# Sequence 0 of a transformer kernel in two halves, its first half ahead with PSUM banks of its own, weights split in gaps, and the first feed-forward tile begun with half a sequence

## The chip, the core and the metric

One NeuronCore of one Trainium2 chip runs the whole program. It has five engines that run side by side and meet at semaphores: TensorE (PE), VectorE (DVE), ScalarE (ACT), GpSimd (POOL) and SyncE (SP, which only issues DMAs here). Each takes its instructions in the order of the program. The metric is the device time of one execution in microseconds, the median of several runs.

## What is computed

There are four sequences of 1024 tokens with 128 features each. The first layer is a block of its own; then come a feed-forward layer, an attention layer, and the same feed-forward layer again. Cut to what matters here (the attention layer is left out, since the change doesn't touch it):

```python
def conv_pool_block(x):                      # layer 1, on layernorm(x)
    h = ln(x, ln_conv_g, ln_conv_b)
    x = x + causal_conv(h, conv_w, 4 taps, 4 groups) + conv_b
    h = ln(x, ln_attn_g, ln_attn_b)
    q, k, v = h @ Wq.T + bq, h @ Wk.T + bk, h @ Wv.T + bv
    pooled_q = cumsum(q, axis=1) / scale     # scale = 1 .. 1024
    pooled_k = cumsum(pooled_q * k, axis=1) / scale
    x = x + pooled_k * v
    h = ln(x, ln_boom_g, ln_boom_b)
    h = gelu(h @ Wb.T + bb)                  # 512 wide
    return x + h @ Wu.T + bu

x = x + conv_pool_block(layernorm(x))
x = x + ffn(layernorm(x))                    # sum over 8 experts of (silu(x@wg) * (x@wu)) @ wd
x = x + attention(layernorm(x))
x = x + ffn(layernorm(x))
```

## The kernel before

Tokens are cut into 8 tiles of 512 (`NT`), two to a sequence, so a sequence is a pair of tiles; a tile is four blocks of 128 tokens. The kernel has three parts in time: a front that takes sequence 0 through layer 1 alone; the first feed-forward layer over four pairs of tiles, with layer 1 of sequence i+1 woven into pair i; and the rest (attention, then the second feed-forward layer beside it), which the change doesn't touch.

**Layer 1 of a sequence** is a chain of named stages, each done for half u = 0 and half u = 1 (512 tokens each). `sequence_step(b, p)` exists once for each engine, and does at position p what the table `AT` puts there. In order: `tok` (normalise tokens), `T1` (PE turns them so that features are the partitions), `copy`, `conv`, `a1`, `T5`, `stats5` (DVE statistics, then four small POOL instructions in `inner_norm`), `norm5`, `T7`, `h2`, then `q`, `cumq` (a running sum on DVE), `k`, `kq`, `cumk`, `v`, `vq`, with POOL's products by the reciprocal positions `rinv` between them, `T9`, `stats9`, `norm9`, `T10`, `h3`, `up` (four matmuls to 512 hidden features), `gelu`, `down` (four back), `y`, `T13`, `x1` (added to `x`). The running sums bind half 1 to the last column of half 0. The chain has PSUM banks 5 and 6 (half u uses bank 5 + u, and the other one in places), so one half's stage waits until the bank is read out.

**The front before** runs these positions for sequence 0 with nothing beside it on PE. Beside it the feed-forward weights are made ready: each of the three 128 x 4096 matrices is needed as a high part `w_hi` (an fp32r rounding, ACT) and a low part `w_lo` (the difference, POOL or DVE). They come in four quarters r = 0 to 3 of 1024 columns (three DMAs a quarter into `raw`), split at positions `SPLIT_AT`: ACT makes all high parts, POOL the low parts of quarters 0 to 2, DVE those of quarter 3. PE waits for all twelve low parts ahead of the first tile. DVE also takes the statistics of sequences 1 to 3 in the front, and POOL their roots (`norms_of_input`).

**The feed-forward layer** has 32 chunks of 128 hidden columns a tile. `pair(i, last)` runs 64 chunks: `gate_up` (three fp32r matmuls each for gate and up) two chunks ahead, `silu` on ACT, `product` on DVE, `h_hi` on ACT, `h_lo` on DVE, and `down` (three matmuls). `NORM_AT` says at which chunk the next tile is normalised. All engines ran pairs 0 to 2 in a hardware loop (`Fori`), and pair 3 written out. One pair takes chunks p = 0 to 63, and position p of sequence i+1 goes with chunk p.

## Time and profile before

| | |
|---|---|
| median of three runs (lowest to highest) | 1820.72 us (1818.81 to 1822.73) |
| the profiled execution, its own time | 1818.75 us |
| its span from first to last instruction | 1817.0 us |
| PE busy | 1704.4 us, 94% of the span |
| DVE, ACT, POOL busy | 69%, 57%, 26% |
| mean granted TensorE clock | 0.982 of full |
| first matmul of the first feed-forward tile | 104.75 us |

The span is cut into the front (0 to 104.75 us), four pairs of some 173 us, and the attention and second feed-forward part. A row of a timeline has the start, the length, the engine, the source line, the operation and its operands; what stands in brackets at its end is the idle time of the engine ahead of it and who ended it. The chain view follows the end of the program back through whatever released each step. A count such as x8 merges equal instructions; the length is then from the first start to the last end. An fp32 matmul of 512 columns shows as two records.

### The profile page before, as it was taken

To read this page: it belongs to the slowest core of one execution; us is meant where nothing else is said; L and a number is where in the kernel's file an instruction comes from. 1 tells how busy PE (TensorE), PEld (TensorE's weight loads), DVE (VectorE), ACT (ScalarE), POOL (GpSimd) and SP (SyncE) were. 2 spreads that over 40 slices of the span, in tenths; PEclk is the share of its full clock that TensorE was granted. 3 is DMA by queue.
4 is the path that set the end of the run, shared out by engine and by line. 5 is a ranking of instruction groups with operands and counts; after the bars stand their busy time and mean duration, and the time that the engine had idled before them with its cause. 6 is when DMAs were issued, how large, how long until landed. Compare 5 with 4: busy or idle time off the path is not lost.

```text
span 1817.0 us, 28722 instructions
## 1 busy us (share of the span) xinstructions
PE 1704.4 (94%) x10264; PEld 1106.2 (61%) x10264; DVE 1250.0 (69%) x2118; ACT 1040.8 (57%) x1694; POOL 477.6 (26%) x651
## 2 busy tenths in 40 slices
PE   4489999999999999988889999999999999999998
PEld 2257777767776877653334555555555555557877
DVE  3558566856675777777777777777777777746665
ACT  3435655574556555456666666556666566665554
POOL 4712000200020012432113444344444344440000
PEclk8699999999999999989999999999999999999999
DMA  5100000000000013232200010000000000010000
GB/s 173 39 1 1 1 1 1 0 0 0 1 0 0 1 61 106 82 100 82 59 25 25 24 36 2 24 24 13 25 23 25 2 24 2 3 30 1 6 7 6
DMA packets 60522, 47.01 MB, mean 26 GB/s; under 512 B 7647, under 2 KB 58222, under 8 KB 60398
## 3 DMA queue, kind: packets, MB, share of 16 engines
q1 hardware_dynamic: 60224, 45.33, 8.5%
q8 instruction: 73, 1.20, 0.3%
q14 instruction: 51, 0.42, 0.1%
q10 hardware_dynamic: 174, 0.07, 0.0%
HBM read 28.20 MB, written 17.17 MB: 25 GB/s over the span
## 4 chain that ended last, share of the span: by engine, by line
PE 83%; DVE 8%; ACT 4%; issue 3%; POOL 2%; DMA 0%; ACTq 0%; DVEq 0%; POOLq 0%
PE ps L1105 8%; PE ps L1068 7%; PE ps L1106 6%; PE ps L1107 6%; PE ps L969 6%; PE ps L971 6%; PE ps L970 6%; PE ps L942 4%; PE ps L1137 4%; PE ps L762 4%; PE ps L911 3%; PE ps L1139 3%; PE ps L1138 3%; PE ps L976 3%; PE ps L977 3%
## 5 line engine op out<-in xcount | busy, mean ns | idle before, releaser
L1434 ACT ACTIVATE pr<-ps 128x1024 f32<-128x1024 f32 (+2 forms) x285 | 267.8, 945 | 187.7 <-PE ps L899 115.7
L1841 DVE TENSOR_TENSOR hid<-sg,ps 128x512 f32<-128x512 f32 x256 | 174.8, 683 | 199.4 <-PE ps L971 155.4
L722 POOL TENSOR_TENSOR h_lo<-hid,h_hi 128x512 fp32r<-128x512 f32 x176 | 225.7, 1282 | 263.5 <-ACT h_hi L1530 259.0
L1440 ACT ACTIVATE sg<-ps 128x512 f32<-128x512 f32 x256 | 153.2, 599 | 244.7 <-PE ps L971 242.6
L1831 DVE TENSOR_REDUCE negp<-ps 128x2 f32<-128x1024 f32 (+2 forms) x224 | 254.6, 1145 | 49.9 <-PE ps L899 29.4
L969 PE MATMUL ps<-xn_hi,w_hi 128*128 128x512 f32 x512 | 226.5, 442 | 1.4 <-DVE xn_lo L1680 1.4
L1105 PE MATMUL ps<-xn_hi,w_hi 128*128 128x512 f32 x512 | 223.3, 436 | 0.7 <-DVE hid L1963 0.5
L1963 DVE SCALAR_TENSOR_TENSOR hid<-sg,ps 128x512 f32<-128x512 f32 x176 | 120.9, 687 | 126.2 <-ACT sg L1520 125.5
L971 PE MATMUL ps<-xn_hi,w_lo 128*128 128x512 f32 x512 | 202.0, 394 | 0.0
L1106 PE MATMUL ps<-xn_lo,w_hi 128*128 128x512 f32 x512 | 201.8, 394 | 0.0
L970 PE MATMUL ps<-xn_lo,w_hi 128*128 128x512 f32 x512 | 201.5, 393 | 0.0
L1107 PE MATMUL ps<-xn_hi,w_lo 128*128 128x512 f32 x512 | 201.3, 393 | 0.0
L1861 DVE TENSOR_TENSOR h_lo<-hid,h_hi 128x512 fp32r<-128x512 f32 x236 | 173.1, 733 | 0.0
L1530 ACT CAST h_hi<-hid 128x512 fp32r<-128x512 f32 x256 | 157.5, 615 | 14.7 <-PE ps L1139 10.2
L1457 ACT CAST h_hi<-hid 128x512 fp32r<-128x512 f32 x256 | 157.3, 614 | 0.6 <-DVE hid L1841 0.4
L1520 ACT ACTIVATE sg<-ps 128x512 f32<-128x512 f32 x176 | 105.4, 599 | 76.8 <-PE ps L1107 75.5
L1068 PE MATMUL ps<-pr,vp 128*9 128x512 f32 (+3 forms) x1376 | 145.3, 495 | 0.0
L942 PEld LDWEIGHTS ps<-qs,ks 63*128 63x128 bf16 x720 | 35.1, 94 | 166.8 <-issue 141.7
L942 PE MATMUL ps<-qs,ks 63*128 63x512 bf16 (+2 forms) x720 | 114.6, 336 | 13.5 <-DVE negp L1831 8.6
L1969 DVE TENSOR_TENSOR hid<-hid,ps 128x512 f32<-128x512 f32 x176 | 120.2, 683 | 6.7 <-PE ps L1107 3.1
L1105 PEld LDWEIGHTS ps<-xn_hi,w_hi 128*128 128x128 f32 x512 | 95.9, 187 | 40.3 <-issue 18.7
L911 PE MATMUL ps<-ks,qs 60*128 60x512 bf16 (+2 forms) x720 | 113.5, 331 | 6.1 <-DVE xn_lo L1953 2.6
(223 smaller groups left out, 3089.9 us busy)
## 6 DMA issues: line engine op xcount, KB each, us to landing
qs<-qd SPq DMA_DIRECT2D x60, 96.0 KB
ks<-kd SPq DMA_DIRECT2D x60, 96.0 KB
kd<-qkp SPq DMA_DIRECT2D x14, 256.0 KB, 2.9
qd<-qkp SPq DMA_DIRECT2D x7, 384.0 KB, 2.6
x<-in_hidden SPq DMA_DIRECT2D x4, 512.0 KB, 6.7
raw<-in_Wg SPq DMA_DIRECT2D x4, 512.0 KB, 4.4
raw<-in_Wu SPq DMA_DIRECT2D x4, 512.0 KB, 5.4
raw<-in_Wd SPq DMA_DIRECT2D x4, 512.0 KB, 6.7
```

Of the source, the lines that this page charges most:

```text
L722: g.tensor_tensor(h_lo[:, q % 2, :], hid[:, q % 4, :], h_hi[:, q % 2, :].bitcast(F32), ALU.subtract).then_inc(FS[1]["hlo_pool"], 1)
L942: mm = pe.matmul(dst[e], k_of(n)[r, hp, j * P:(j + 1) * P], q_of(n)[r, hp, from_q:from_q + w], start=True, stop=st not in MASKED)
L969: pe.matmul(dst, w_hi[m][:, w], xn_hi[:, h, :], start=True, stop=False)
L970: pe.matmul(dst, w_hi[m][:, w], xn_lo[:, h, :], start=False, stop=False)
L971: pe.matmul(dst, w_lo[m][:, w], xn_hi[:, h, :], start=False, stop=True).then_inc(f[sig], 1)
L1068: mm = pe.matmul(ps[32 * h:32 * h + HD + 1, O_BANK, from_q:NT], vp[:, n % 2, j, h, :], pr_of(n, st)[:, h, 0:NT - from_q], start=(j == 0), ...
L1105: pe.matmul(dst, w_hi[m][:, w], xn_hi[:, h, :], start=True, stop=False)
L1106: pe.matmul(dst, w_hi[m][:, w], xn_lo[:, h, :], start=False, stop=False)
L1107: pe.matmul(dst, w_lo[m][:, w], xn_hi[:, h, :], start=False, stop=True).then_inc(f[sig], 1)
L1434: a.activation(pr_of(n, st)[:].rearrange("p (e a) q -> p e a q", e=2)[:, :, hps[0]:hps[-1] + 1, 0:WIDTH[st]], heads(buf, hps, WIDTH[st]), ...
L1831: v.tensor_reduce(to[:, :, hps[0]:hps[-1] + 1, i % SUB], heads(buf, hps, JOB_WIDTH[k]), AX.X, ALU.max, negate=True).then_inc(T["reduced"], 1)
L1841: v.tensor_tensor(hid[:, c % 4, :], sg[:, c % 2, :], bank(2 + c % 2), ALU.mult).then_inc(f["prod"], 1)
```

## The change

**Order.** In the front each engine now has sequence 0's stages written out one by one (`first_step(name, u)`), half 0 ahead of half 1. Half 0 (called `ahead` in the code) has banks 0, 1 and 4 of its own, banks 0 to 3 for its four `up` matmuls, and a tile `gel_first` into which ACT puts the gelu with the bias in one instruction for each matmul. The feed-forward begins when half 0 is through: half 1's last stages (`up`, the gelu, `down`, `y`, `T13`, `x1`) stand around the first chunks. Pair 0 is written out as well (the loop has pairs 1 and 2), with sequence 1's positions six chunks later (`SHIFT_FIRST`) and tile 2's norm at chunk 20 of the second half.

**Loads and setup.** `x` of sequence 0 comes as two DMAs of 256 KB, and the other sequences' `x` after the small matrices and two quarters of the weights. There are two root chains of 4 blocks for sequence 0 where there was one of 8. ACT, not POOL, spreads the convolution weights. The reciprocal of the positions is taken in four quarters.

**Weights.** The low parts of quarter 0 are POOL's (two) and DVE's (one); those of quarter 1 are DVE's; those of quarters 2 and 3 are POOL's, quarter 3 inside pair 0. PE no longer waits for all twelve, but for quarter 0 ahead of the tile and for quarter r ahead of chunk 8r.

The constants, SP's queue, and POOL:

```diff
-NORM_AT = (10, 16)
...
-SPLIT_AT = (5, 10, 19, 27)
+SHIFT_FIRST = 6
+NORM_AT = {"first": (10, 20), "middle": (10, 16), "last": (13, None)}
+HIGH_LATE = 5
...
-                    sp.wait_ge(s["split_lo"], (r - 1) * 3)
+            def load_weights(r):
                 for m in range(3):
                     n = 2 if m < 2 else BLK
-                    sp.dma_start(raw[r % 2][m][:, :].rearrange("p (n f) -> p n f", n=n),
-                                 ffn_src[m][:, r * n:(r + 1) * n, :]).then_inc(s[f"raw_loaded{r % 2}"], 16)
+                    sp.dma_start(raw[r][m][:, :].rearrange("p (n f) -> p n f", n=n),
+                                 ffn_src[m][:, r * n:(r + 1) * n, :]).then_inc(s[f"raw_loaded{min(r, 1)}"], 16)
+
+            load_weights(0)
+            load_weights(1)
+            for b in range(1, B):
+                sp.dma_start(xs(b * BLK, BLK).rearrange("p (n d) -> p n d", d=D),
+                             x_blk[:, b * BLK:(b + 1) * BLK, :]).then_inc(s["x_rest_loaded"], 16)
+            for r in (2, 3):
+                sp.wait_ge(s[f"split_lo{r - 1}"], 3)
+                load_weights(r)
             attention_loads(sp)
...
+            def low_part(r, m):
+                pool.wait_ge(s[f"split_hi{r}"], m + 1)
+                g.tensor_tensor(w_lo[m][:, r * S:(r + 1) * S], raw[r][m][:],
+                                w_hi[m][:, r * S:(r + 1) * S].bitcast(F32), ALU.subtract).then_inc(s[f"split_lo{r}"], 1)
+
+            norms_of_input(0, SUB)
+            norms_of_input(SUB, BLK)
+            low_part(0, 0)
+            low_part(0, 1)
+            sequence_step(0, only("stats5", 0))
+            sequence_step(0, only("stats5", 1))
+            pool.wait_ge(s["rinv_ready"], 3)
+            sequence_step(0, only("cumq", 0))
+            sequence_step(0, only("cumk", 0))
+            sequence_step(0, only("vq", 0))
+            pool.wait_ge(s["rinv_ready"], 5)
+            sequence_step(0, only("cumq", 1))
+            sequence_step(0, only("stats9", 0))
+            sequence_step(0, only("cumk", 1))
+            sequence_step(0, only("vq", 1))
+            sequence_step(0, only("stats9", 1))

...
+                low_part(2, 0)
+                low_part(2, 1)
                 norm(0)
-                with pool.Fori(0, TILES // 2 - 1) as i:
-                    for p in range(2 * CH):
-                        sequence_step(i + 1, p)
-                        if p % CH == NORM_AT[p // CH]:
-                            norm(i * 2 + (p // CH + 1))
+                low_part(2, 2)
+                norms_of_input(BLK, B * BLK)
+                for m in range(3):
+                    low_part(3, m)
+                pair(0, "first")
```

PE, the front's order and the start of the tile:

```diff
+            for t in range(T_CONV, T_IN):
+                weight_T(t)
+            pe.wait_ge(s["small_loaded"], 16 * N_SMALL)
+            pe.transpose(bank(2)[:, 0:PAR_ROWS], prow[:, :],
+                         ident[0:PAR_ROWS, 0:PAR_ROWS]).then_inc(s["par_T"], 1)
+            for t in range(T_COUNT):
+                if not T_CONV <= t < T_IN:
+                    mm = weight_T(t)
             mm.then_inc(s["wraw_T"], 1)
-            pe.transpose(bank(7)[:, 0:PAR_ROWS], prow[:, :], ident[0:PAR_ROWS, 0:PAR_ROWS]).then_inc(s["par_T"], 1)
...
-            for p in range(AT["T1"][0] + 1, 2 * CH):
-                sequence_step(0, p, first=True)
+            first_step("T1", 0)
+            first_step("conv", 0)
+            first_step("T1", 1)
+            first_step("T5", 0)
+            first_step("conv", 1)
+            first_step("T7", 0)
+            first_step("T5", 1)
+            first_step("q", 0)
+            first_step("k", 0)
+            first_step("v", 0)
+            first_step("T7", 1)
+            first_step("q", 1)
+            first_step("k", 1)
+            first_step("T9", 0)
+            first_step("v", 1)
+            first_step("T10", 0)
+            for c in range(4):
+                first_step("up", 0, c)
+            first_step("T9", 1)
+            for c in range(4):
+                first_step("down", 0, c)
+            first_step("T13", 0)
+            first_step("T10", 1)
+            first_step("up", 1, 0)
+            first_step("up", 1, 1)

...
+                                if kind == "first" and p + 2 in (8, 16, 24):
+                                    pe.wait_ge(s[f"split_lo{(p + 2) // 8}"], 3)
                                 gate_up(h if c + 2 < CH else 1 - h, (c + 2) % CH)
...
                 transpose4(bank(7), ntok).then_inc(f["xT"], 1)
+                first_step("up", 1, 2)
+                first_step("up", 1, 3)
+                pe.wait_ge(s["split_lo0"], 3)
                 pe.wait_ge(f["xlo"], 1)
                 gate_up(0, 0)
                 gate_up(0, 1)
-                with pe.Fori(0, TILES // 2 - 1) as i:
-                    pair(i, False)
-                pair(TILES // 2 - 1, True)
+                for c in range(4):
+                    first_step("down", 1, c)
+                pair(0, "first")
+                with pe.Fori(1, TILES // 2 - 1) as i:
```

ACT and DVE, the front's order and what stands in the first pair:

```diff
+            act.wait_ge(s["par_ready"], 1)
+            first_step("copy", 0)
+            projections()
+            first_step("tok", 1)
+            for m in range(3):
+                high_part(0, m)
+            first_step("copy", 1)
+            first_step("h2", 0)
+            for m in range(3):
+                high_part(1, m)
+            first_step("norm5", 1)
+            first_step("h2", 1)
+            first_step("h3", 0)
+            for c in range(4):
+                first_step("up", 0, c)
+            for m in range(3):
+                high_part(2, m)
+            first_step("norm9", 1)
+            first_step("h3", 1)

...
                                 act.wait_ge(f["xT"], t + 2)
                                 split_input(1 - h)
+                            if kind == "first" and HIGH_LATE <= h * CH + c < HIGH_LATE + 3:
+                                high_part(3, c - HIGH_LATE)
...
                 split_input(0)
+                first_step("gelu", 1)
                 act.wait_ge(f["gate"], 1)
                 silu(0)
...
+            for u in range(2):
+                dve.wait_ge(s[f"x_loaded{u}"], 16)
+                stats_of_input(u * SUB, u * SUB + SUB)
+            positions()
+            quarter_of_positions(0)
...
+            first_step("tok", 1)
+            projections()
+            quarter_of_positions(3)
+            dve.wait_ge(s["par_ready"], 1)
+            first_step("a1", 0)
+            first_step("copy", 1)
+            first_step("stats5", 0)
+            low_part(0, 2)
+            first_step("norm5", 0)
+            first_step("a1", 1)
+            first_step("stats5", 1)
+            first_step("cumq", 0)
+            low_part(1, 0)
+            first_step("kq", 0)
+            first_step("cumk", 0)
+            low_part(1, 1)
+            first_step("vq", 0)
+            first_step("cumq", 1)
+            low_part(1, 2)
+            first_step("stats9", 0)
+            first_step("kq", 1)
+            first_step("norm9", 0)
+            first_step("cumk", 1)
+            first_step("vq", 1)
+            dve.wait_ge(s["x_rest_loaded"], 16 * (B - 1))
+            stats_of_input(BLK, 2 * BLK + SUB)
+            first_step("stats9", 1)
+            stats_of_input(2 * BLK + SUB, B * BLK)
+            first_step("y", 0)
+            first_step("x1", 0)
+            dve.wait_ge(s["a_x1"], 1)
+            first_norm(FS[0], 0)
+            first_norm(FS[0], 3)
+            first_step("hid1", 1, 0)
+            first_step("hid1", 1, 1)
...
+                                first_step(("y", "x1")[c], 1)
+                            if kind == "first" and h * CH + c == SHIFT_FIRST:
+                                dve.wait_ge(s["a_lnx"], 28)
                             if not last:
-                                sequence_step(i + 1, h * CH + c)
```

What this does to the engines' queues is seen at three places. On PE, the end of the front and the first chunks, before (ps is PSUM, work holds the hidden activations, a0T the transposed sequence):

```order
L831 MATMUL ps<-h2T,wt 128x512 x8
L838 MATMUL ps<-work,wt 128x512 x4
L762 MATMUL ps<-ident,a0T 128x128 x4
L838 MATMUL ps<-work,wt 128x512 x4
L762 MATMUL ps<-ident,a0T 128x128 x4
L762 MATMUL ps<-ident,ntok 128x128 x4
L969 MATMUL ps<-xn_hi,w_hi 128x512
```

and now:

```order
L872 MATMUL ps<-h2T,wt 128x512 x4
L793 MATMUL ps<-ident,a0T 128x128 x4
L881 MATMUL ps<-gel_first,wt 128x512 x4
L793 MATMUL ps<-ident,a0T 128x128 x4
L793 MATMUL ps<-ident,work 128x128 x4
L872 MATMUL ps<-h2T,wt 128x512 x2
L793 MATMUL ps<-ident,ntok 128x128 x4
L872 MATMUL ps<-h2T,wt 128x512 x2
L1041 MATMUL ps<-xn_hi,w_hi 128x512
```

The tile's transposes (ntok) stand before half 1's last two `up` matmuls, and half 1's four `down` matmuls and its T13 have moved behind the first chunks. On POOL, the pooling products of the front (L613, L616, L620) and the low parts of quarters 1 and 2, before:

```order
L633 TENSOR_TENSOR w_lo<-raw,w_hi 128x1024 x3
L613 TENSOR_TENSOR work<-work,rinv 128x512
L616 TENSOR_TENSOR work<-work,rinv 128x512
L613 TENSOR_TENSOR work<-work,rinv 128x512
L633 TENSOR_TENSOR w_lo<-raw,w_hi 128x1024 x3
L620 TENSOR_TENSOR a0T<-a0T,work 128x512
L616 TENSOR_TENSOR work<-work,rinv 128x512
```

and now:

```order
L628 TENSOR_TENSOR work<-work,rinv 128x512
L631 TENSOR_TENSOR work<-work,rinv 128x512
L635 TENSOR_TENSOR a0T<-a0T,work 128x512
L628 TENSOR_TENSOR work<-work,rinv 128x512
L613 TENSOR_TENSOR lna<-mva,eps 128x4
L614 TENSOR_TENSOR lna<-lna,half 128x4
L615 TENSOR_TENSOR lna<-mva,lna 128x4
L616 TENSOR_TENSOR lna<-zeros,lna 128x4
L631 TENSOR_TENSOR work<-work,rinv 128x512
L635 TENSOR_TENSOR a0T<-a0T,work 128x512
```

No low part stands between the pooling products any more, and half 0's second root (L613 to L616) stands ahead of half 1's products. On DVE, the last instructions ahead of the first product (`hid`), now:

```order
L1900 SCALAR_TENSOR_TENSOR a0T<-ps,par,a0T 128x512
L1904 TENSOR_TENSOR x<-x,ps 128x512
L1784 BN_STATS st<-x 128x6 x4
L1786 MEMSET fence 128x1
L1788 BN_AGGR mv<-st 128x2 x4
L1792 TENSOR_SCALAR ntok<-x,mv,lnw 128x128 x4
L1896 TENSOR_SCALAR work<-ps,par 128x512 x2
L2057 MEMSET x 128x512
L2058 MEMSET ps 128x512
L1807 TENSOR_TENSOR xn_lo<-ps,xn_hi 128x512
L1896 TENSOR_SCALAR work<-ps,par 128x512 x2
L2007 TENSOR_TENSOR hid<-sg,ps 128x512 x2
```

Half 1's hidden columns (L1896) stand around the first tile's xn_lo, where before they were done long ahead of it.

## Rows read from the trace of the kernel before

**Rows 1.** The page: busy time of the engines.

```profile
PE 1704.4 (94%) x10264; PEld 1106.2 (61%) x10264; DVE 1250.0 (69%) x2118; ACT 1040.8 (57%) x1694; POOL 477.6 (26%) x651
```

**Rows 2.** Windows: stretch, length, busy (count) by engine, PEclk, DMA share, GB/s.

```profile
0.00:104.75 104.75, 50.00 (x140) 25.62 (x140) 48.89 (x155) 38.25 (x60) 58.80 (x70) 0.80 0.31 92
104.75:281.84 177.09, 173.93 (x720) 129.26 (x721) 114.66 (x224) 99.17 (x176) 16.57 (x26) 0.99 0.00 1
26.00:33.00 7.00, 6.12 (x13) 3.17 (x12) 0.69 (x1) 5.57 (x7) 1.82 (x1) 0.50 0.00 0
62.00:84.00 22.00, 8.01 (x21) 4.79 (x22) 11.59 (x69) 5.61 (x12) 12.71 (x15) 0.50 0.01 1
105.50:108.40 2.90, 2.90 (x8) 2.30 (x7) 0.69 (x1) 0.60 (x1) 0.00 (x0) 0.50 0.00 0
```

**Rows 3.** The chain that ended last, 0 to 110 us: start, length, what.

```profile
0.81 4.97 DMA x<-in_hidden
...
28.27 9.70 PE ps L785 x16
...
54.17 1.24 DVE work L1741
...
58.05 7.82 POOL w_lo L633 x3
...
80.19 9.61 PE ps L831 x16
...
90.72 3.69 PE ps L838 x8
...
104.01 0.70 DVE xn_lo L1680
...
104.75 0.50 PE ps L969
```

**Rows 4.** Timeline of PE.

```profile
16.01 1.94 PE L762 MATMUL ps<-ident,work 128*128 128x128 f32 x8 [16.01 <-DVE work L1710]
...
123.87 3.60 PE L785 MATMUL ps<-hT,wt 128*128 128x512 f32 x8
```

**Rows 5.** Timeline of DVE.

```profile
68.29 0.89 DVE L1694 BATCH_NORM_STATS2 sta<-ps 128x6 f32<-128x128 f32 x4 [6.86 <-PE ps L762]
...
163.31 0.68 DVE L1861 TENSOR_TENSOR h_lo<-hid,h_hi 128x512 fp32r<-128x512 f32 x1
...
168.75 1.40 DVE L1861 TENSOR_TENSOR h_lo<-hid,h_hi 128x512 fp32r<-128x512 f32 x1
```

**Rows 6.** Timeline of POOL.

```profile
44.33 6.97 POOL L633 TENSOR_TENSOR w_lo<-raw,w_hi 128x1024 fp32r<-128x1024 f32 x3
51.59 1.26 POOL L613 TENSOR_TENSOR work<-work,rinv 128x512 f32<-128x512 f32 x1 [0.29 <-DVE work L1728]
...
69.68 0.20 POOL L598 TENSOR_TENSOR lna<-mva,eps 128x4 f32<-128x4 f32 x1 [1.37 <-DVE mva L1698]
69.96 1.02 POOL L599 TENSOR_TENSOR lna<-lna,half 128x4 f32<-128x4 f32 x1
...
83.17 5.04 POOL L576 TENSOR_TENSOR lnx<-tmpx,half 128x24 f32<-128x24 f32 x1
...
168.33 1.27 POOL L613 TENSOR_TENSOR work<-work,rinv 128x512 f32<-128x512 f32 x1 [1.82 <-DVE work L1728]
```

**Rows 7.** Timeline of ACT.

```profile
21.03 1.95 ACT L1345 COPY wt<-ps 128x512 f32<-128x512 f32 x4 [3.63 <-PE ps L857]
...
90.60 1.91 ACT L1390 ACTIVATE work<-work 128x2048 f32<-128x2048 f32 x1 [0.75 <-DVE work L1756]
...
103.99 1.28 ACT L1440 ACT_TABLE_LOAD   x1
106.13 0.60 ACT L1440 ACTIVATE sg<-ps 128x512 f32<-128x512 f32 x1 [0.85 <-PE ps L971]
```

**Rows 8.** DMA traffic between 2.5 and 10 us.

```profile
DMA packets 4355, 2.18 MB, mean 291 GB/s; under 512 B 100, under 2 KB 4355, under 8 KB 4355
```

More of the change, by code:

```diff
@@ L242, in build @@
         with ExitStack() as one:
+            sb("under_gelu", [P, 3 * S], F32, one)
+            gel_first = sb("gel_first", [P, 4, NT], F32, one)
+        with ExitStack() as one:
             v_first = sb("v_first", [P, BLK, D], F32, one)
@@ L1012, in pair @@
                                 maxima_T(0)
-                            if c == norm_at(h, last) + 4 and not end:
+                            if not end and c == NORM_AT[kind][h] + 4:
                                 pe.wait_ge(f["xadd"], t + 1)
@@ L1330, in attention @@
                 rest_of_ffn()
-            pe.wait_ge(s["split_lo"], 12)
             ffn(FS[0])
@@ L1891, in ffn @@
                 product(0)
-                with dve.Fori(0, TILES // 2 - 1) as i:
-                    pair(i, False)
-                pair(TILES // 2 - 1, True)
+                pair(0, "first")
+                with dve.Fori(1, TILES // 2 - 1) as i:
+                    pair(i, "middle")
+                pair(TILES // 2 - 1, "last")
                 dve.wait_ge(G["rest"], LAST * 2)
```

407 lines of the change are left out of this document (219 added, 188 removed).

## The prediction

> **What bounds the kernel now.** I read the page first: PE is busy for 94% of the span [rows 1], so outside the front only less PE work or less waiting could help. The windows then show where PE does wait. In the front, 0 to 104.75 us, it is busy for 50.0 of 104.75 us, and in the first pair for 173.9 of 177.1 [rows 2]. So there is a pool of some 55 us that lies almost whole in the front, and the change works on the front. The chain shows what the front consists of [rows 3]: eight convolution matmuls together (9.70 us), the pooling chain that goes from engine to engine, 7.82 us of POOL's low parts of the weights in the midst of it, then eight `up` matmuls (9.61), two times four `down` (3.69 for the first), and the feed-forward's first matmul at 104.75. All of that is done for both halves of the sequence before a tile begins, though the tile needs one half. The windows also give the clock: the granted clock stands at 0.50, that is 1.2 GHz, in 26 to 33, in 62 to 84 and again in 105.5 to 108.4 us [rows 2], after stretches in which PE was idle or sparse. At 1.2 GHz an fp32 matmul of 512 columns takes some 1.7 us; at 2.4 GHz four of them take 3.60 or less, 0.86 each [rows 4].
>
> **The walk through the new front.** The price of the new front is an order, so I walk through it, each instruction with its row's duration, 0.05 to 0.1 us for a hand-over, and each engine in its program order. The times are of half 0's chain.
> - Loads. In 2.5 to 10 us the queues move 291 GB/s [rows 8], and 512 KB of x land at 5.78 [rows 3]. The small matrices (0.98 MB) have 0.52 MB of x ahead of them, not 2.1 MB: with 1.5 us from last byte to signal they land at 9.2. x's first 256 KB land at about 4.9, and its root chain on POOL is through at 10.6.
> - Weights. PE has 16 transposes behind the load, then 8 for T1, 1.94 for eight [rows 4]: 13.0 and 14. ACT's four copies (1.95 [rows 7]) end at 15.1, `hT` at 15.9.
> - `conv` of half 0: four matmuls, 3.4 us at 2.4 GHz, to 19.4; `a1` to 20.3; T5 behind half 1's T1 to 20.9; statistics (1.4 us from the first statistics at 68.29 to POOL's start at 69.68 [rows 5, 6]) behind a copy, to 22.5. POOL is then in quarter 0's two low parts (6.97 us for three [rows 6]) until 23.9, and its root (0.2 + 1.02 [rows 6]) is there at 25.3. `norm5` on DVE to 26.4, T7, `h2`, and `q` starts at 27.9.
> - Pooling. The running sum waits for half 1's statistics on DVE, to 30.3; POOL's product (1.26 [rows 6]) waits for half 1's root and ends at 32.7; `kq`, `cumk` (1.24 [rows 3]) to 34.8; POOL's next product is held up by a low part on DVE, 37.1; `vq` 38.0; a2 39.3.
> - T9 to `h3` as in the rows of before, 46.4. Four `up` matmuls, the first three at 1.2 GHz, to 52.0; the four `down`, 3.69 at the most [rows 3], to 56. Then `y`, behind 12 statistics of the other sequences on DVE, 58.3; T13, `x1` 59.7; statistics, root, `norm` 63.7; `xn_hi` 65.0; `xn_lo` behind two of half 1's `hid` and two memsets, 66.9.
>
> The first tile so begins at 66.9 in the walk. The same walk through the order of before gives 102 to 106, by where the clock changes, for the 104.75 of the trace; single stages were up to 2 us short. I add 2 and take 69, with 66 to 72 as what the clock alone can do. **First term: 104.75 - 69 = 35.8 us less front.**
>
> **What moves into the first pair.** Before it took 177.1 us [rows 2].
> - Half 1's four `down` are on PE now, 3.4 us, and its T13, 0.5. Its last two `up` (1.7) stand ahead of the first chunk, and lie under DVE's `xn_lo`.
> - ACT's gelu of half 1 (1.91) now stands ahead of the first `silu` and of its table load (1.28, at 103.99 before) [rows 7]. The first `silu` so comes 4.8 us after the first matmul, not 1.4 (106.13 against 104.75 [rows 3, 7]). PE has the `down` matmuls to do in the meantime, but waits 0.7 for the gelu and some for the first product: 1.3.
> - The clock: before, the pair starts with 3.7 us at 1.2 GHz [rows 2]; now PE has been dense for a while, which gives back 1.7.
> - POOL's remaining low parts (four of 2.3 us [rows 6]) and its roots for 24 blocks (12.6 us, of which 5.04 is one instruction [rows 6]) run beside the first chunks. Row 168.75 shows `h_lo` at 1.40 us, which began beside a product of POOL's that ended at 169.60, where it takes 0.68 with POOL idle [rows 5, 6]. I put 1 us on PE for four such meetings, since most of it lies in slack: none at the least, 4 x 2.3 at the most. The Trainium skill ("SBUF — State Buffer", section on SBUF's two separate sides) says that GpSimd and a DVE instruction with two SBUF inputs take the shared port pair for a whole instruction; by that rule DVE's own low parts of quarters 0 and 1 can be kept back by POOL too. The trace agrees in this one meeting; without such a lock the walk would be 2 us shorter, with it at every meeting 5 us longer.
> - Sequence 1's six chunks of delay cost nothing: its last position, 46, now falls on chunk 52 of 64, and the next tile's norm stands at chunk 52 behind it. ACT's high parts of quarter 3 (3 x 1.04) wait for a DMA that is issued when quarter 2 is split, 65 us, and lands some 7 us later, before chunk 5.
>
> **Second term: +3.4 + 0.5 + 1.3 - 1.7 + 1.0 = +4.5, rounded to 4 since part of the gelu's wait lies under the others.** The pair then ends at 69 + 177.1 + 4 = 250.1 where it ended at 281.84 [rows 2]: 31.7 less. What follows is the same instructions and only earlier. The new queues leave SP nothing to hold up: its next DMA of the attention part is hundreds of us away.
>
> **The sum.** The profiled execution took 1818.75 us; less 31.7 it is 1787.0. The median of the three runs, 1820.72, is 2 us above it, which gives 1789. I forecast 1788.
>
> **The rivals.**
> - *Smaller gain: the front stays sparse for the clock.* The walk has 2.4 GHz for both `conv` and for `q` and `k`, though PE is idle in half of that stretch; [rows 2] show 0.50 all through 62 to 84 with 8 us of work in 22. If half 0 runs at 1.2 GHz throughout, `conv` costs 3.4 more, the other's `conv` ahead of T7 and half of `q` and `k` 2.6, the transposes 1, `up` and `down` 4 more: the start moves to 78 to 80 and the time to 1794 to 1799. Against it: PE is busier here than in 62 to 84. 20%.
> - *Larger gain.* The added 2 us aren't needed, the load lands early, `h_lo` meets nothing: start at 64, pair +2, 1780 to 1783. 12%.
> - *The gain is given back in the first pair.* PE now waits for quarters 1, 2 and 3 ahead of chunks 8, 16 and 24, and DVE waits at chunk 6 for the 24 roots, with all products behind it. POOL makes both: roots at about 10 us after the start against 18 for chunk 6, quarter 3 at about 28 us against 56 for chunk 24. Only a POOL queue 8 us later would be felt at all, and one some 40 us later would leave no gain: 1817 to 1824. 3%.
> - *Slower: the clock stays low in the first pair.* This is one place, the first pair, where PE now starts with the sequence's rest in between. At 1.2 GHz a chunk's nine matmuls take 3.8 us, not 2.1. It decides from some 20 chunks on at the low clock, since 20 x 1.77 are the 35 us; the whole pair so would give 1900. Against it: before, the clock rose 3.7 us after the dense matmuls began, though the front ahead of it was sparser. 3%.
>
> The forecast itself (start between 66 and 72) has the remaining 62%.
>
> **How the numbers follow.** 0.2% is 3.6 us, about what a measurement of this kernel can tell from no change. Forecast, smaller and larger gain are all faster by more than that: 94%; no change 3%, slower 3%. The forecast's own range is 1783 to 1793. The range given reaches down over half of the larger gain and up to most of the smaller: 1781 to 1798.
>
> **What the profile will show, and what would prove me wrong.** The first xn_hi matmul between 66 and 72 us; no chain row of POOL w_lo between the pooling products; the granted clock at 2.4 GHz at the first chunk; a first silu nearly 5 us behind the first matmul; the end of chunk 64 near 250; h_lo of over 1.4 us beside POOL's L639 in chunks 0 to 12. I am wrong if the first matmul stands beyond 75, if PE waits for a split_lo or DVE at chunk 6 for the roots, or if the second or third pair is not the 173 us that it was.

## The result and the profile after

| | before | after |
|---|---|---|
| median (lowest to highest) | 1820.06 us (1818.81 to 1822.73), 4 runs | 1790.59 us (1790.13 to 1791.45), 4 runs |
| ratio after to before, 95% interval | | 0.9837 (0.982 to 0.9854) |
| profiled execution: own time, span | 1818.75, 1817.0 us | 1790.59, 1788.9 us |
| first feed-forward matmul | 104.75 us | 70.23 us |
| first pair, from that matmul to its end | 177.1 us | 185.3 us |

The change makes the kernel 29.5 us faster by the medians, 28.1 us by the two profiled spans. I had forecast 1788.0 us in 1781 to 1798.

The page of the changed kernel, busy time of the engines, answers to [rows 1]: PE has the same work in a shorter span.

```profile
PE 1703.1 (95%) x10264; PEld 1105.3 (62%) x10264; DVE 1260.6 (70%) x2129; ACT 1038.5 (58%) x1689; POOL 477.5 (27%) x654
```

Windows of the changed kernel, columns as in [rows 2]: the front, the first pair, and two stretches at the lower clock.

```profile
0.00:70.23 70.23, 43.32 (x129) 21.48 (x129) 52.31 (x163) 29.40 (x50) 44.95 (x62) 0.88 0.42 126
70.23:255.52 185.29, 179.52 (x734) 132.24 (x733) 122.61 (x229) 105.07 (x180) 30.20 (x38) 0.98 0.02 5
66.00:71.00 5.00, 4.23 (x10) 2.44 (x11) 4.41 (x10) 0.59 (x1) 4.70 (x4) 0.66 0.84 242
99.00:105.00 6.00, 6.00 (x21) 4.99 (x20) 4.84 (x8) 3.71 (x8) 1.74 (x1) 0.56 0.01 3
```

The front shrank by 34.5 us, and PE is idle in it for 26.9 us where it was for 54.8. The pair grew by 8.2: 5.6 of that is more PE time (half 1's `down`, and 6 us at a granted clock of 0.56), the rest is waiting. The chain shows how the new front runs (start, length, what):

```profile
32.66 1.27 POOL work L628
34.03 0.76 DVE work L1875
34.81 1.24 DVE work L1882
36.12 2.17 POOL work L631
...
47.12 6.64 PE ps L872 x8
...
57.56 4.66 POOL w_lo L639 x2
...
63.59 3.14 DVE ntok L1792 x4
66.77 1.12 PE ps L793 x4
67.89 2.92 PE ps L872 x4
```

The pooling products now follow each other without one of POOL's low parts between them, where 7.82 us of POOL's `w_lo` stood in [rows 3]. New is the end: four `ntok` instructions take 3.14 us. DVE's timeline shows the same four and what happened around chunk 6 (columns as in [rows 5]):

```profile
60.18 0.69 DVE L1904 TENSOR_TENSOR x<-x,ps 128x512 f32<-128x512 f32 x1 [0.75 <-PE ps L793]
60.91 0.87 DVE L1784 BATCH_NORM_STATS2 st<-x 128x6 f32<-128x128 f32 x4
...
63.59 3.12 DVE L1792 TENSOR_SCALAR ntok<-x,mv,lnw 128x128 f32<-128x128 f32 x4 [1.40 <-POOL lnw L663]
...
90.61 1.77 DVE L2028 TENSOR_TENSOR h_lo<-hid,h_hi 128x512 fp32r<-128x512 f32 x1
92.31 2.36 DVE L1831 COPY lns<-lnx 128x32 f32<-128x32 f32 x1
...
98.14 3.20 DVE L1844 TENSOR_SCALAR work<-x,lns 128x128 f32<-128x128 f32 x4
```

POOL's timeline of the same kernel, at the same places:

```profile
63.53 2.34 POOL L639 TENSOR_TENSOR w_lo<-raw,w_hi 128x1024 fp32r<-128x1024 f32 x1
...
89.41 5.21 POOL L639 TENSOR_TENSOR w_lo<-raw,w_hi 128x1024 fp32r<-128x1024 f32 x2 [12.66 <-ACT w_hi L1496]
98.36 2.38 POOL L639 TENSOR_TENSOR w_lo<-raw,w_hi 128x1024 fp32r<-128x1024 f32 x1 [3.74 <-ACT w_hi L1496]
```

Each slow DVE instruction lies beside one of POOL's low parts: `ntok` began 0.06 us after one, and the `lns` copy, which takes 0.17 us in later pairs, ended where POOL's two did (94.6). The waits of PE between 70 and 250 us (us in total, times, longest) show who paid:

```profile
PE ps L1048 <- DVE h_lo L2028: 4.7, 4, 3.5
```

The longest, 3.5 us, is that of chunk 7 at 98.37 (the expectations below call it chunk 8), behind sequence 1's tokens on DVE and ACT, which were behind the `lns` copy; the clock fell to 1.2 GHz right behind it, in 99 to 105.

Where the later pairs stand is read from the copies into `yS`, one at the first chunk of each pair. ACT's timeline of the kernel before:

```profile
109.69 0.59 ACT L1460 COPY yS<-ps 128x512 f32<-128x512 f32 x1
...
282.04 0.59 ACT L1460 COPY yS<-ps 128x512 f32<-128x512 f32 x1 [0.28 <-PE ps L978]
...
455.55 0.59 ACT L1460 COPY yS<-ps 128x512 f32<-128x512 f32 x1 [0.28 <-PE ps L978]
```

and of the changed one:

```profile
76.79 0.58 ACT L1577 COPY yS<-ps 128x512 f32<-128x512 f32 x1
...
255.72 0.59 ACT L1577 COPY yS<-ps 128x512 f32<-128x512 f32 x1 [0.28 <-PE ps L1050]
...
427.72 0.59 ACT L1577 COPY yS<-ps 128x512 f32<-128x512 f32 x1 [0.28 <-PE ps L1050]
```

The first pair took 172.35 us between its copies and now takes 178.93; the second 173.51 and now 172.00. The books: start -34.52, from it to the first copy +1.62, first pair +6.58, second pair -1.51, all the rest -0.27, together -28.1 us.

### The profile page after: what moved, and what is told of

Same layout as the page of the kernel before. It is cut to its first block, busy times and chain, and to the rows that moved or that the text cites. A ratio compares the mean times of both kernels' runs of the same rounds, so it can differ in the third digit from the quotient of the medians.

```text
span 1788.9 us, 28441 instructions
## 1 busy us (share of the span) xinstructions
PE 1703.1 (95%) x10264; PEld 1105.3 (62%) x10264; DVE 1260.6 (70%) x2129; ACT 1038.5 (58%) x1689; POOL 477.5 (27%) x654
## 4 chain that ended last, share of the span: by engine, by line
PE 83%; DVE 8%; ACT 4%; issue 3%; POOL 2%; ACTq 0%; SPq 0%; DMA 0%; DVEq 0%; POOLq 0%
PE ps L1188 8%; PE ps L1151 7%; PE ps L1189 6%; PE ps L1190 6%; PE ps L1041 6%; PE ps L1043 6%; PE ps L1042 6%; PE ps L1014 4%; PE ps L1220 4%; PE ps L983 3%; PE ps L793 3%; PE ps L1222 3%; PE ps L1221 3%; PE ps L1048 3%; PE ps L1050 3%
```

## The experiments

Theory: the gain is the start, made of four parts (half 0 ahead in PE's order, the tile begun with half a sequence, the loads, no low part between the products); what is given back comes mostly from POOL's low parts, each of which holds back DVE instructions that read and write SBUF. (The change has more parts than these four: half 0's banks, the two root chains, the convolution weights spread by ACT and the reciprocal in quarters were not undone one by one.) Rivals: a single part (the low parts out of the chain) makes nearly all of the gain; and the low parts are harmless, the pair being longer for half 1's work alone. The code behind the first pair is the same in all variants of the changed kernel and took 1531.8 to 1535.3 us in their profiled executions, so an effect of 1 or 2 us is read from its place in the trace, and the medians only confirm it.

| | first matmul | end of first pair (copy into yS) | median, us | ratio to before (95%) |
|---|---|---|---|---|
| changed kernel | 70.23 | 255.72 | 1790.59 | 0.9837 (0.982 to 0.9854) |
| e1, ntok clear | 68.69 | 252.56 | 1788.32 | 0.9831 (0.9818 to 0.9845) |
| e2, quarter 3 early | 70.13 | 250.86 | 1789.22 | 0.9831 (0.9817 to 0.9845) |
| e3, quarter 3 late | 69.75 | 251.98 | 1789.33 | 0.9836 (0.9823 to 0.985) |
| e5, e1 and e2 | 67.95 | 249.42 | 1785.21 | 0.9807 (0.9792 to 0.9821) |
| e9, e5 in pieces | 68.65 | 248.09 | 1782.23 | 0.9801 (0.9787 to 0.9814) |
| e10, quarter 3 on DVE | 68.40 | 247.67 | 1783.26 | 0.9799 (0.9786 to 0.9812) |
| e6, whole sequence | 81.28 | 262.63 | 1797.95 | 0.9878 (0.9863 to 0.9893) |
| e8, x first | 74.62 | 258.46 | 1795.03 | 0.9862 (0.9846 to 0.9878) |
| e11, low parts in the chain | 73.46 | 257.69 | 1795.55 | 0.9873 (0.9858 to 0.9888) |
| e12, PE's old order | 84.81 | 270.36 | 1805.42 | 0.9928 (0.9913 to 0.9943) |
| e4, before unrolled | | 282.10 | 1818.36 | 0.9995 (0.9986 to 1.0004) |
| e7, before, quarter 2 late | 101.46 | 279.71 | 1814.66 | 0.9966 (0.9953 to 0.9979) |

Each group of runs had the kernel before beside it, with a median of 1820.06 us for the changed kernel, 1819.65 for e1 to e4, 1820.43 for e5 to e8 and 1818.43 for e9 to e12. So across groups the ratios are compared, not the medians.

### e1: POOL's low part kept off ntok

```diff
                 norm(0)
+                pool.wait_ge(f["norm"], SUB)
                 low_part(2, 2)
```

> The changed kernel, with one wait added: POOL's third low part of quarter 2 (2.34 us, begun at 63.53) waits until DVE has normalised the tile's tokens (ntok L1792, 63.59, 3.12 us for four). Theory: the low part held the shared SBUF port of DVE and POOL, so that the four ntok took 3.12 us instead of 1.11; without the meeting they take 1.1 us, the first feed-forward matmul comes 1.5 to 2.5 us earlier (at about 68.2, not 70.23), and the time falls to 1788 to 1789 from 1790.6. Rival: ntok is slow for another reason (a row of x read right after it was written), or half 1's up matmuls set the start: ntok stays at 3 us, or the first matmul stays at 70, and the time doesn't move.

Measured: DVE's group of this tile, and PE's first feed-forward matmul in the timeline:

```profile
L1793 DVE TENSOR_SCALAR ntok<-x,mv,lnw x4: 341/342/346, 64.4 to 65.2; 128x128 f32<-128x128 f32 x4
```

```profile
68.69 0.47 PE L1042 MATMUL ps<-xn_hi,w_hi 128*128 128x512 f32 x1 [0.48 <-DVE xn_lo L1808]
```

All four `ntok` take 0.34 us, and the matmul comes 1.54 us earlier, with the clock at 1.00 in 66 to 71 instead of 0.66. The low part held `ntok` back, as the theory had it. The meeting cost more than 1.54 us, since in this execution half 0's `x1` began 0.80 us later (60.98 against 60.18). From `x1` to the first matmul it takes 7.71 us in e1, e5 and e9, where `ntok` meets no low part, and 10.05 in the changed kernel; in e3, e8 and e11, where it meets one but the clock behind it is at 1.00, it takes 9.7. So the meeting costs 2.0 us, and 0.3 more with the clock. PE's wait of 3.5 us at chunk 7 is still there; this time no stretch at 1.2 GHz followed it (99 to 105 stood at 1.00), so the wait alone doesn't decide the clock. Without that stretch the pair takes 177.50 us between its copies instead of 178.93: the fall was worth 1.4 us, less than the 2.6 that 6 us at a clock of 0.56 suggest, because a slower PE waited less for `h_hi` (0.7 us in all instead of 1.9).

### e2 and e3: the low parts of quarter 3 moved

```diff
-HIGH_LATE = 5
+HIGH_LATE = 1
```

> The changed kernel, with ACT's high parts of quarter 3 at chunks 1 to 3 instead of 5 to 7, so that POOL's three low parts of quarter 3 run at about 78 to 85 us, ahead of sequence 1's first DVE work at chunk 6. Theory: PE's longest wait of the first pair (3.5 us at chunk 8, and 1.2 GHz from 99 to 105 behind it) comes from these low parts holding DVE's port in the very chunks in which DVE also has sequence 1's lns copy (2.36 us instead of 0.18) and four tok instructions; moved away the lns copy takes 0.2 us, the wait falls below 1.5 us, and the time by 2 to 5 us, to 1786 to 1789. Rival: the low parts cost the same wherever they run in the pair, since each holds back an h_lo by up to 2.3 us in a pair where PE has no slack: the wait only moves to chunks 2 to 5 and the time stays within 1 us of 1790.6. A third way: the high parts wait for the quarter's DMA (it landed at about 73) and ACT holds up the second chunk; then 1791 or more.

For e3 POOL takes them inside the pair:

```diff
-HIGH_LATE = 5
+HIGH_LATE = 12
...
-                for m in range(3):
-                    low_part(3, m)
                 pair(0, "first")
...
                         if p % CH == NORM_AT[kind][p // CH]:
                             norm(i * 2 + (p // CH + 1))
+                        if kind == "first" and p == 16:
+                            for m in range(3):
+                                low_part(3, m)
```

> The changed kernel, with ACT's high parts of quarter 3 at chunks 12 to 14 and POOL's three low parts behind both roots of sequence 1's stats5 (chunk 16), where DVE has only products and h_lo beside them. Theory (the double load on DVE at chunk 6 makes the wait): lns copy back at 0.2 us, PE's longest wait in the first pair below 1.5 us, time 1786 to 1789. Rival (a low part costs the same anywhere): a wait of 2 to 3.5 us at chunks 16 to 20, time within 1 us of 1790.6. If the low parts come too late for chunk 24, PE waits for them there and the time rises above 1791.

Measured in e2, DVE's group of the copy, and PE's waits:

```profile
L1831 DVE COPY lns<-lnx x1: 174/174/174, 92.4 to 92.4; 128x32 f32<-128x32 f32 x1
```

```profile
PE ps L1048 <- DVE h_lo L2028: 1.7, 3, 1.0
```

and in e3 PE's waits:

```profile
PE ps L1049 <- DVE h_lo L2029: 2.4, 3, 1.0
```

In both the copy is back at 0.17 to 0.18 us and the longest wait at 1.0. The first pair takes 174.17 us in e2 and 175.86 in e3 between its copies, against 178.93: the meeting with sequence 1's work was the dearer part, 4.8 us by e2. The low parts cost something beside `h_lo` alone too: against the 172.89 of e10, where POOL has none in the pair, e2 is 1.3 us longer and e3 3.0. The end of the pair comes 4.9 and 3.7 us earlier. The medians show 1.4 and 1.3 us, just short of the 1786 to 1789 expected, and the ratios lie within the interval of the changed kernel, so by time alone neither is told from it.

### e4: pair 0 written out, in the kernel before

```diff
-                with pe.Fori(0, TILES // 2 - 1) as i:
+                pair(0, False)
+                with pe.Fori(1, TILES // 2 - 1) as i:
```

(and the same on the other engines)

> The kernel before, with pair 0 written out and the hardware loop over pairs 1 and 2 alone: this part of the change by itself. Theory from the traces: the way from one turn of the loop into the next costs 1.5 us (a pair took 173.5 us behind a turn, 172.0 in the changed kernel where pair 1 is the loop's first), so one turn fewer gives 1.5 us: 1818.5 against 1820.1. Rival: entering the loop from written-out code costs what the turn did, and pair 1 was shorter for another reason: 1820 and no difference, or a little slower for code that must be fetched.

Measured, ACT's timeline:

```profile
282.10 0.59 ACT L1464 COPY yS<-ps 128x512 f32<-128x512 f32 x1 [0.28 <-PE ps L981]
...
453.73 0.59 ACT L1464 COPY yS<-ps 128x512 f32<-128x512 f32 x1 [0.28 <-PE ps L981]
```

The second pair takes 171.63 us where it took 173.51 behind a turn of the loop. By place the theory holds. The time, 1.3 us less, has 1 in its interval, and the two profiled spans are both 1817.0 us: the part behind the first layer's last pair, where the code is the same, was 2.1 us longer here.

### e5: both edits

The diffs of e1 and e2 together.

> The changed kernel with the edits of both single tests: POOL's low part of quarter 2 behind ntok, and quarter 3's high parts at chunks 1 to 3. Theory: the two meetings are independent, so the gains add: first matmul at about 68.7 (alone: 68.69), end of the first pair at 255.72 - 3.16 - 4.86 = 247.7 by the two single profiles, at the latest 249, and the time 1785 to 1787 against 1790.6. Rival: the earlier start brings the low parts of quarter 3 (POOL's queue is 1 us later here) onto other chunks and gives part back: pair end at 250 to 252, 1787.5 to 1789.

Measured: 1785.21 us, as expected, but the pair ends at 249.42, not 247.7. DVE's timeline shows the price of the new place:

```profile
79.37 2.24 DVE L2029 TENSOR_TENSOR h_lo<-hid,h_hi 128x512 fp32r<-128x512 f32 x1
81.53 0.68 DVE L2008 TENSOR_TENSOR hid<-sg,ps 128x512 f32<-128x512 f32 x1
82.13 2.29 DVE L2029 TENSOR_TENSOR h_lo<-hid,h_hi 128x512 fp32r<-128x512 f32 x1
...
84.94 2.29 DVE L2029 TENSOR_TENSOR h_lo<-hid,h_hi 128x512 fp32r<-128x512 f32 x1
```

Three `h_lo` (SBUF in, SBUF out) are held back by 1.6 us each, while `hid`, with one input from PSUM, stays at 0.68 in the same stretch.

### e6: the first tile begun with the whole sequence

On every engine half 1's last stages stand ahead of the tile; on PE:

```diff
-                pe.wait_ge(f["norm"], SUB)
-                transpose4(bank(7), ntok).then_inc(f["xT"], 1)
                 first_step("up", 1, 2)
                 first_step("up", 1, 3)
+                for c in range(4):
+                    first_step("down", 1, c)
+                first_step("T13", 1)
+                pe.wait_ge(f["norm"], SUB)
+                transpose4(bank(7), ntok).then_inc(f["xT"], 1)
                 pe.wait_ge(s["split_lo0"], 3)
                 pe.wait_ge(f["xlo"], 1)
                 gate_up(0, 0)
                 gate_up(0, 1)
-                for c in range(4):
-                    first_step("down", 1, c)
```

> The changed kernel, but the first tile begun only when the whole sequence is through layer 1: half 1's hid, gelu, down, y, T13 and x1 stand ahead of the tile's normalisation on every engine. Half 0 still runs ahead with its own banks. Theory (the head start of half a sequence is a real part of the gain, about 12 us at the start, of which 6 are work that PE does later anyway): first matmul at 80 to 84, not 70.2; the first pair 5 to 8 us shorter; time 1794 to 1799 against 1790.6, so 5 to 8 us of the 29.5 come from beginning with half a sequence. Rival: PE's work is the same either way and the front's gaps are only moved, so the time stays within 2 us of 1790.6.

Measured: first matmul at 81.28, 11.05 us later; 1797.95 us, 7.4 more. The pair, from that matmul to the second copy, is 4.1 us shorter, not 5 to 8. The theory holds: a quarter of the gain is the early tile. The edit also freed `ntok` of its meeting (1.11 us for four), so the early tile alone is worth up to 2 us more than this, which no run shows by itself.

### e7: the kernel before, quarter 2's low parts behind the products

```diff
-                if p in SPLIT_AT[:3]:
-                    r = SPLIT_AT.index(p)
+                if p in (5, 10, 27):
+                    r = (5, 10, 27).index(p)
```

> The kernel before with one edit: POOL's three low parts of quarter 2 (7.86 us at 58.00, between two pooling products, on the chain) run at position 27, behind the last product, and ACT's high parts stay where they were. Theory: the chain loses most of the 7.8 us; the first matmul comes at 97 to 99, not 104.75, and the time falls to 1812.5 to 1815 from 1820: so a quarter of the change's gain needs neither half ahead nor the early tile. Rival: the pooling chain of half 0 wasn't what half 1 waited for (its q and scan set the pace), or the low parts only push POOL's roots for 24 blocks and the tile's norm back by the same 7 us: first matmul above 102, time above 1817.

Measured: 1814.66 us, within the theory's range, and the first matmul at 101.46, between theory and rival. The chain:

```profile
67.78 1.27 POOL a0T L620
...
77.90 5.88 DVE w_lo L1791 x3
83.78 0.67 DVE work L1756
```

The last product, at 71.76 before, comes 4.0 us earlier; then DVE's own three low parts of quarter 3 stand ahead of `hid` and take over. They are longer than they were, 5.88 us and not 3.54. DVE's timeline before, and POOL's in e7:

```profile
81.81 3.54 DVE L1791 TENSOR_TENSOR w_lo<-raw,w_hi 128x1024 fp32r<-128x1024 f32 x3
```

```profile
73.58 7.94 POOL L633 TENSOR_TENSOR w_lo<-raw,w_hi 128x1024 fp32r<-128x1024 f32 x3
```

The edit has put POOL's low parts beside DVE's, and so made a meeting of its own, 2.3 us on DVE; PE then waits 1.06 us for the `hid` behind it. Taking the 7.82 us out of the chain gave 3.3 us at the start, and would have given perhaps 1 us more without that meeting, by that wait (an estimate).

### e8: the other sequences' x loaded first

```diff
+            for b in range(1, B):
+                sp.dma_start(xs(b * BLK, BLK).rearrange("p (n d) -> p n d", d=D),
+                             x_blk[:, b * BLK:(b + 1) * BLK, :]).then_inc(s["x_rest_loaded"], 16)
             load_matrices(sp)
```

(and not behind the weights)

> The changed kernel with the loads back in the old order: the 1.5 MB of x of sequences 1 to 3 ahead of the small matrices and the weights. Theory (my walk has the small matrices as what PE's first transposes wait for): at 291 GB/s they land 5.4 us later, at about 14.8, the first matmul comes at 75 to 76, and the time rises by 4.5 to 6 us to 1795 to 1796.5. Rival: half 0's chain has slack behind x's statistics and roots (through at about 10.6), or POOL's and DVE's low parts set the pace further on, so that less than 3 us is felt: below 1793.5.

Measured, PE's waits from 10 us on:

```profile
PE ps L906 <- DMA wraw<-in_w_out: 4.7, 1, 4.7
```

First matmul at 74.62, 4.4 us later, just under the 75 expected, and 1795.03 us, 4.4 more: nearly the whole wait of 4.7 us for the load reaches the start and the end.

### e9 and e10: quarter 3's low parts in pieces, or on DVE

Both start from e5. In e9 POOL has two instructions of 512 columns for one of 1024:

```diff
-                    low_part(3, m)
+                    pool.wait_ge(s["split_hi3"], m + 1)
+                    for lo in (3 * S, 3 * S + NT):
+                        ins = g.tensor_tensor(w_lo[m][:, lo:lo + NT], raw[3][m][:, lo - 3 * S:lo - 3 * S + NT],
+                                              w_hi[m][:, lo:lo + NT].bitcast(F32), ALU.subtract)
+                    ins.then_inc(s["split_lo3"], 1)
```

> The kernel of e5_both, with each of POOL's three low parts of quarter 3 written as two instructions of 512 columns instead of one of 1024. Theory: what holds DVE back is one POOL instruction for its whole length, so with pieces of half the length the three h_lo in chunks 1 to 4, 2.24 to 2.29 us long in e5, take at most 1.9 us each and mostly 1.3; the first pair (175.1 us between the two copies into yS) gets 0.5 to 1.5 us shorter, the time 1784 to 1785.5 against 1785.2. Rival: POOL holds the port from the first to the last of a run of instructions that follow each other without a wait: h_lo stays at 2.3 us, the pair at 175, the time at 1785.2 or a little more for the added instructions.

and in e10 DVE takes them:

```diff
+                            if kind == "first" and 2 <= h * CH + c < 5:
+                                low_part(3, c - 2)
```

> The kernel of e5_both, with the three low parts of quarter 3 on DVE, one each at chunks 2, 3 and 4, instead of on POOL. Theory: on DVE such an instruction takes 1.2 us and holds nobody, against 1.6 us that each of POOL's takes from DVE, so the pair gets about 1 us shorter: 1784 to 1785.2. Rival: DVE has only 0.7 us to spare in a chunk (product 0.69 and h_lo 0.68 of 2.1), and work of its own adds up where a held-up instruction is absorbed: PE waits for h_lo over 1.5 us and the time is 1785.5 to 1787.

Measured in e9, DVE's timeline:

```profile
80.07 1.15 DVE L2033 TENSOR_TENSOR h_lo<-hid,h_hi 128x512 fp32r<-128x512 f32 x1
...
82.15 0.76 DVE L2033 TENSOR_TENSOR h_lo<-hid,h_hi 128x512 fp32r<-128x512 f32 x1
...
84.33 1.53 DVE L2033 TENSOR_TENSOR h_lo<-hid,h_hi 128x512 fp32r<-128x512 f32 x1
```

and POOL's:

```profile
79.37 9.38 POOL L722 TENSOR_TENSOR w_lo<-raw,w_hi 128x512 fp32r<-128x512 f32 x6
```

In e10, DVE's timeline:

```profile
79.83 0.68 DVE L2027 TENSOR_TENSOR h_lo<-hid,h_hi 128x512 fp32r<-128x512 f32 x1
80.43 1.22 DVE L1911 TENSOR_TENSOR w_lo<-raw,w_hi 128x1024 fp32r<-128x1024 f32 x1
```

`h_lo` is held for at most 0.85 us in e9, so the hold ends with the instruction, not with the run of them. The pair takes 173.06 us in e9 and 172.89 in e10, against 175.10 in e5. Both beat the changed kernel, with intervals that don't overlap its own: 2.0% off the kernel before instead of 1.6%. Which of the two is better isn't settled, and by time neither is told from e5 (0.9807, whose interval overlaps both): by place the pair is 2 us shorter. Both medians were under the 1784 that I had as their best, but the kernel before was 2.0 us faster in this group too. Of e9's profiled span, 3.6 us below e5's, 1.3 lie up to the end of the first pair and 2.3 behind it, where the code is the same.

### e11: quarter 1's low parts between the products again

```diff
             sequence_step(0, only("cumq", 0))
+            for m in range(3):
+                low_part(1, m)
             sequence_step(0, only("cumk", 0))
```

(and not on DVE)

> The changed kernel, but quarter 1's three low parts (DVE's, 1.2 us each) done by POOL again, in the place of the old ones: between half 0's first and second pooling product. Theory: POOL's second product comes some 5 to 6 us later (three of 2.33 us less the 1.5 us in which POOL waited there, and what DVE gains), the first matmul at 74 to 76, the time 1794 to 1796.5. Rival: DVE was as much in the way with its three (each stood in front of a stage of the chain), so the move costs under 3 us: first matmul below 73, below 1793.5.

Measured, POOL's timeline:

```profile
33.93 7.86 POOL L639 TENSOR_TENSOR w_lo<-raw,w_hi 128x1024 fp32r<-128x1024 f32 x3
41.76 1.25 POOL L631 TENSOR_TENSOR work<-work,rinv 128x512 f32<-128x512 f32 x1
```

The product came 5.6 us later, but the first matmul only 3.2, between theory and rival. One us of the difference is the product itself, which met no low part of DVE's (1.25 us long, not 2.17); that DVE without its three low parts made up the rest is argued, not shown. In reverse, DVE's running sum beside POOL's low parts (34.86) took 2.50 us where it takes 1.22 in the changed kernel. The time is 5.0 us higher by the medians and 6.5 by the ratios, the profiled execution's (the shortest of the four) 2.0; the size stays between 2 and 6.5 us.

### e12: PE in the old order

```diff
-            first_step("T5", 0)
             first_step("conv", 1)
-            first_step("T7", 0)
+            first_step("T5", 0)
             first_step("T5", 1)
+            first_step("T7", 0)
+            first_step("T7", 1)
             first_step("q", 0)
             first_step("k", 0)
             first_step("v", 0)
-            first_step("T7", 1)
             first_step("q", 1)
             first_step("k", 1)
             first_step("T9", 0)
             first_step("v", 1)
+            first_step("T9", 1)
             first_step("T10", 0)
...
-            first_step("T9", 1)
```

> The changed kernel with PE's front in the old order, half 1's stage right behind half 0's: conv of half 1 ahead of T5 of half 0, T7 of half 1 ahead of q, T9 of half 1 ahead of T10 of half 0. Banks, loads, the other engines' orders and the early tile stay. Theory (PE's order is what lets half 0 run ahead): T5 of half 0 waits 3.4 us behind conv of half 1, T10 some 5 us behind half 1's pooling: first matmul at 77 to 80, time 1796 to 1800. Rival: POOL's and DVE's chains set the pace and PE's order is only free room: first matmul within 3 us of 70.2, time below 1793.5.

Measured, PE's timeline:

```profile
31.49 1.12 PE L793 MATMUL ps<-ident,a0T 128*128 128x128 f32 x4 [5.71 <-DVE a0T L1853]
...
38.55 1.12 PE L793 MATMUL ps<-ident,work 128*128 128x128 f32 x4 [5.10 <-ACT work L1468]
...
61.56 1.11 PE L793 MATMUL ps<-ident,a0T 128*128 128x128 f32 x4 [7.26 <-POOL a0T L635]
```

The direction is the theory's, the price nearly double: 84.81, 14.6 us later, and 1805.42 us. Not PE's extra work is dear, but that each of half 0's stages now waits for half 1's stage on another engine: T7 stands behind T5 of half 1, which waits for its `a1` (5.7 us), `q` behind T7 of half 1, which waits for its `norm5` (5.1), and T10 behind T9 of half 1, which waits for its last product (7.3), and much of it at 1.2 GHz (the granted clock is 0.50 in 60 to 66).

## Why the prediction was right, and where it was off

**Start 69 (66 to 72): right, in part by luck.** It was 70.23, 3.3 us behind the walk's own 66.9. The walk's times are ends of stages: `h3` ended at 47.08 (walk 46.4), `y` at 59.43 (58.3) and `x1` at 60.87 (59.7), so up to there it was 1.2 us short. The rest is the meeting at `ntok`, 2.3 us with the clock behind it, which the walk didn't price. The 2 us that I had added for stages that come out short covered most of both. The first term, 35.8, was 34.5. Without the meeting the start is 68.65 in e9, 68.69 in e1 and 67.95 in e5.

**What made the start.** The single edits that undo one part move it by 14.6 (PE's order), 11.0 (early tile), 4.4 (loads) and 3.2 us (low parts in the chain). They sum to 33.3 of 34.5, though that parts add isn't shown. The 7.82 us in [rows 3] looked like the plain gain, and e11 and e7 give 3.2 and 3.3 us for them, each with a side effect named there. What half 0's banks of its own are worth alone wasn't tried.

**First pair +4: the step that was mis-sized.** It was +8.2. Of its terms, `down` and T13, the gelu with its table load ahead of the first `silu` (74.84, 4.6 us behind the first matmul) came as said. With its meetings cut short, e9 has from its first matmul to the end 6.38 + 173.06 us, 2.1 us more than the 177.3 of before counted the same way, less than the 3.5 that my terms without contention gave. The port term, 1.0 (0 to 9.2), is what failed in size: in the pair it was 178.93 - 173.06 = 5.9 us, of it 3.1 in PE's waits for `h_lo` (4.7 against 1.6) and about 2.6 in 6 us at a clock of 0.56. Where the clock didn't fall it was 4.4 (177.50 - 173.06, e1). With `ntok`, 2.3, it is 8.2 in all. I had counted four meetings with `h_lo`, in slack, and not that POOL also holds instructions with a single SBUF input, nor that quarter 3 fell on the chunks in which DVE has sequence 1's tokens too.

**Unpriced: the turn of the loop.** Writing pair 0 out took 1.5 us from pair 1. I had named a second pair other than 173 us as a sign of being wrong, and it was 172.00; pair 2 took 173.49, as said. Against the 1787.0 us of my sum, the profiled execution had +1.2 at the start, +4.2 in the first pair, -1.5 in the second and -0.3 behind it, and came to 1790.59. The 1 us that I had put on top for the median wasn't there, since this execution is the median. So 1790.6 against 1788 hides errors of opposite sign.

**The rivals.** The front was not too sparse for the clock (granted 0.88 over the front, 0.80 before), so the smaller gain fell; what shortened my gain lay where the third rival had it, in the first pair, but came by DVE instructions held back and not by a wait for `split_lo` or the roots, and at a size between the forecast and that rival. The larger gain's condition in the pair was nearly made by e9, with `h_lo` met only in pieces and the pair at +2.1; its start at 64 was not (68.65). That e9's 1782.23 lies inside the 1780 to 1783 that I had for it is luck: the loop gave 1.5 that I hadn't priced, and by its ratio it would be 1783.8 beside the 1820.06 us of the result. PE waited for no split_lo, and DVE not for the roots at chunk 6 (done at 76.75 against 92). The clock at the first chunk came but for one instruction: the first xn_hi matmul took 0.80 us and the ones behind it 0.39. The `h_lo` of over 1.4 us beside POOL's low parts came too (1.77 at 90.61). The end of chunk 64 near 250 was wrong by 5.5 us.

**The page's rule.** The Trainium skill ("SBUF — State Buffer", "Who interferes with whom") says that GpSimd and a DVE instruction in a 2-port mode or with two SBUF inputs exclude each other for a whole instruction. The runs agree for the low parts: in e9 half the instruction holds `h_lo` for at most 0.85 us, not 1.6. They differ for POOL's power, whose inputs are in SBUF: it took 4.17 us and held no `h_lo` (0.69, last section); there the measurement decides. The same section names copy and tensor_scalar among those that can take the shared pair, which `ntok` and `lns` bear out; my walk had used its two-input half alone.

## What to carry to other kernels

Before moving work to GpSimd, list which VectorE instructions that read and write SBUF run beside it, one-input copies and tensor_scalar as well; keep it off the path with a wait, cut it into shorter instructions, or leave it on VectorE. In a chain that goes from engine to engine, the order in which the fast engine takes its stages can cost more than any instruction on it. And when an operation sits on the chain, ask what ends next to it, and what it will meet in its new place, before counting its length as gain: 7.8 us gave 3.3.

## What the runs showed of the hardware

- Beside a POOL low part these DVE instructions, with all tensors in SBUF, were held: two inputs (`h_lo`, 2.29 us instead of 0.68; the running sum, 2.50 instead of 1.22 in e11), one input (`ntok` and tok, one of four at 2.3 to 2.4 instead of 0.34; the 128x32 copy, 2.36 instead of 0.17). Not held were the statistics of SBUF tokens (60.91, 0.87 for four, beside a low part of 57.56 to 62.22), the add of `x` with one input from PSUM (60.18, 0.69) and `hid` (0.68 in e5).
- The hold goes both ways: POOL's product at 36.12 took 2.17 us behind DVE's low part, not 1.26 [rows 6]. DVE's had begun at 35.96 and took 1.20.
- POOL's power of 128x24 didn't hold an `h_lo` that began inside it. POOL's and DVE's timelines of e5:

```profile
72.68 4.17 POOL L595 TENSOR_TENSOR tmpx<-tmpx,half 128x24 f32<-128x24 f32 x1
```

```profile
74.45 0.69 DVE L2029 TENSOR_TENSOR h_lo<-hid,h_hi 128x512 fp32r<-128x512 f32 x1
```

- A turn of the hardware loop, which four engines go through, cost 1.5 to 1.9 us (173.51 against 172.00 and 171.63).
- After the same wait of 3.5 us PE's clock fell to 1.2 GHz in the changed kernel and in e12, and stayed at 2.4 in e1, e6, e8 and e11. Why is open.
